# Places of one batch alternated with the route of the next, in a fused cross-attention and mixture-of-experts kernel

## The chip, the cores and the metric

The kernel runs on one core of one Trainium2 chip. The metric is the device time of one execution in microseconds (us), as the median of several runs. A core has five engines that run their own instruction streams side by side and meet only at semaphores: TensorE (PE) for matrix products, VectorE (DVE), ScalarE (ACT), GpSimd (POOL) and SyncE (SP), which here only starts DMA transfers. POOL starts transfers too, among them the indexed ones.

## What is computed

Four batches of 512 rows by 256 (`x`), a context of four times 1601 rows by 512, and a list of patch lengths. First the rows are normed and joined with a projection and with a decayed sum over the context rows, which each row of `x` picks by an index worked out from the patch lengths. Then comes a mixture of eight experts, of which every row uses the two with the largest logits:

```python
x = x + _L0_xattn_ref(_layernorm(x), ctx_2048, mask_BxS2_if0, W_in, b_in, g_res, g_init)
x = x + _L0_ffn_ref(_layernorm(x), gate_w, w1, w3, w2)

# in _L0_xattn_ref: rmsnorm, projection, then
plug = jnp.clip(jnp.cumsum(boundary_mask, axis=1) - 1, 0, plen - 1)
depool_out = depool[jnp.arange(bsz)[:, None], plug]        # depool: decayed running sum

# in _L0_ffn_ref: E = 8, TOP_K = 2
probs = jax.nn.softmax(jnp.einsum('btd,de->bte', x, gate_w))
expert_weights, expert_indices = jax.lax.top_k(probs, TOP_K)
for i in range(E):
    h = silu(x @ w1[i]) * (x @ w3[i])
    out = out + (h @ w2[i]) * wi[..., None]                # wi: weight of expert i, or 0
```

## The kernel before

Every batch is four tiles of 128 rows (`TPB` is 4, `B` is 4). The program has two parts. The **head**, up to 104 us, does everything per batch and ends in a table: which rows each expert gets, in blocks of 128. The **steps** after it go over the blocks, at most 39 (37 here), and PE is busy in them nearly without a gap. The whole head must be over before the first step, since the table needs the counts of all four batches.

There is no scheduler: each engine's instructions stand in the order in which the code issues them, and an engine that waits for a semaphore holds all that stands behind. So the order of the calls in each engine's block is the schedule. A wait of an engine on its own last instruction is written out too (`wait_ge` on the count that the instruction adds to).

The parts of the head that matter here:

- DVE, from line 1019: `position(b)` makes 13 compares of 128x128 that mark where batch `b`'s patches end; `stats_first(b)` takes the statistics of `x`; `norm_first(b)` writes the scaled context rows `hp` (the tile `hmul` in the profile); `depooled(b)` takes the decayed sums out of PE's bank; `plugs()` and `plugs_end()` make the index list `plugi` for all batches; `second(b)` joins the gathered rows `dg` and the projection into `x_all` and takes statistics again; `norm_second(b)` hands on the scale with which ACT then writes `z`.
- DVE's routing: `route(b)` copies the logits, finds the top two experts and marks them (`oh`, `picked`); `places(b)` works out the weights and each row's place in its expert's list, a chain of small instructions in which nearly each waits for the one before; `place_rows(b)` (line 1002) makes eight compares of 128x128 (`lo_hot`, shown as `ctx_sb` in the profile, whose memory it reuses). Then nine further small steps, issued through `tbl`, each of which waits for the last.
- PE, from line 1429: `boundaries(b)` needs `position(b)`; `plugs()` needs `bmask`; `depool(b)` makes the decayed sums from `hp`; `turned(b)` and `router(b)` are transposes; `through_win(b)` is the projection; `logits_of(b)` and `ranks(b)` feed `route` and `places`; `lists` makes the row lists from `lo_hot`.
- POOL, from line 508: `pow1(b)` and `pow2(b)` are the powers of -1/2 for the two norms, `gather(b)` fetches `dg` with four indexed transfers of 128 rows. They stand in one queue, so a power stands behind the gathers ahead of it.
- ACT: squares of the context, the two norms, copies of the transposes, the exponential of the logits' gap.

## Time and profile before

| | us |
|---|---|
| median of 3 runs | 457.45 |
| lowest and highest | 455.36, 458.01 |
| the profiled execution, its device time | 460.46 |
| its span in the trace | 458.9 |
| first matmul of the first step | 103.98 |
| PE busy in the span | 398.2 (87%) |

The profiled execution took 3.0 us more than the median, and 1.56 us of its own time lie outside the span. All times of the rows below count from the start of that span. An idle time in square brackets is the engine's wait ahead of an instruction, with what ended it. A row that stands for several instructions starts with the first of them and gives their time in sum.

### The profile page before, as it was taken

To read this page: it belongs to the slowest core of one execution; us is meant where nothing else is said; L and a number is where in the kernel's file an instruction comes from. 1 tells how busy PE (TensorE), PEld (TensorE's weight loads), DVE (VectorE), ACT (ScalarE), POOL (GpSimd) and SP (SyncE) were. 2 spreads that over 40 slices of the span, in tenths; PEclk is the share of its full clock that TensorE was granted. 3 is DMA by queue.
4 is the path that set the end of the run, shared out by engine and by line. 5 is a ranking of instruction groups with operands and counts; after the bars stand their busy time and mean duration, and the time that the engine had idled before them with its cause. 6 is when DMAs were issued, how large, how long until landed. Compare 5 with 4: busy or idle time off the path is not lost.

```text
span 458.9 us, 11850 instructions
## 1 busy us (share of the span) xinstructions
PE 398.2 (87%) x2269; PEld 339.4 (74%) x2270; DVE 313.5 (68%) x835; ACT 193.4 (42%) x334; POOL 204.6 (45%) x215
## 2 busy tenths in 40 slices
PE   0769895239899999999999999999999999799973
PEld 0548674127678888888888888888888888688862
DVE  7977789989685577547767764766776557736550
ACT  2547347002643455335635543463563345443320
POOL 6436456123343465235645553565565232504222
PEclk9979996557999999999999999999999999979977
DMA  6944996601895789557886986797797645525532
GB/s 188 341 161 138 296 365 193 223 25 56 253 270 171 194 250 251 182 156 205 254 255 189 270 256 158 196 277 239 194 282 242 156 138 162 147 69 153 142 105 24
DMA packets 79130, 89.79 MB, mean 196 GB/s; under 512 B 6871, under 2 KB 59351, under 8 KB 79111
## 3 DMA queue, kind: packets, MB, share of 16 engines
q1 hardware_dynamic: 64279, 55.23, 37.1%
q0 software_dynamic: 14832, 34.35, 29.5%
q8 instruction: 6, 0.10, 0.1%
q14 instruction: 13, 0.11, 0.1%
HBM read 58.76 MB, written 30.80 MB: 195 GB/s over the span
## 4 chain that ended last, share of the span: by engine, by line
PE 71%; DVE 15%; issue 5%; POOL 4%; DMA 1%; ACT 1%; DVEq 1%; ACTq 0%; POOLq 0%; SPq 0%
PE bank L1477 68%; POOL dg L499 3%; DVE onehot_lo L852 2%; PE bank L1484 2%; DVE ctx_sb L1008 1%; ACT split L342 1%; DMA out<-yblk,itok 1%; POOL rs L489 1%; PE bank L1425 1%; DVE hmul L901 1%; DVE st L927 1%; DVE st L874 1%; DVE x_all L924 1%; DVE topi L949 1%; DVE x_all L918 1%
## 5 line engine op out<-in xcount | busy, mean ns | idle before, releaser
L1477 PE MATMUL bank<-split,xT_hi 128*128 x592 | 171.7, 412 | 7.4 <-DVE split L348 3.3
L1477 PEld LDWEIGHTS bank<-split,xT_hi 128*128 128x128 f32 x592 | 108.6, 193 | 31.7 <-issue 9.4
L1477 PEld LDWEIGHTS bank<-split,hT 128*128 128x128 f32 x888 | 112.9, 193 | 4.3 <-ACT yblk L714 0.9
L1477 PE MATMUL bank<-split,hT 128*128 (+1 forms) x888 | 114.2, 285 | 0.8 <-ACT yblk L714 0.7
L544 POOL DMA_INDIRECT out<-yblk,itok x37 | 76.6, 2071 | 75.0 <-ACT yblk L714 67.4
L707 ACT ACTIVATE gact<-bank 128x512 f32<-128x512 f32 x74 | 44.3, 599 | 148.4 <-PE bank L1477 148.4
L1207 DVE TENSOR_TENSOR hmul<-gact,bank 128x512 f32<-128x512 f32 x74 | 50.8, 687 | 78.5 <-ACT gact L707 78.3
L1477 PE MATMUL bank<-split,xT_lo 128*128 x296 | 94.8, 402 | 0.0
L536 POOL DMA_INDIRECT xblk<-z_rows,gidx x40 | 41.3, 1032 | 90.7 <-DVE gidx L1246 83.1
L348 DVE TENSOR_TENSOR split<-raw,split x22 | 50.4, 2293 | 28.4 <-ACT split L342 28.4
L1477 PEld LDWEIGHTS bank<-split,xT_lo 128*128 128x128 f32 x296 | 57.1, 193 | 13.8
L1215 DVE STREAM_TRANSPOSE swap_in<-hmul 128x512 f32<-128x512 f32 x74 | 52.7, 712 | 4.4
L1223 DVE TENSOR_TENSOR hT<-swap_out,hT 128x512 fp32r<-128x512 f32 x72 | 48.9, 680 | 1.5
L342 ACT ACTIVATE split<-raw (+1 forms) x24 | 45.8, 1914 | 9.7 <-issue 6.3
L281 POOL DMA_DIRECT2D raw<-in_L_ffn_w x56 | 38.0, 683 | 26.0 <-issue 26.0
L695 ACT ACTIVATE hT<-swap_out 128x512 fp32r<-128x512 f32 x72 | 45.1, 627 | 2.3 <-issue 2.3
L714 ACT ACTIVATE yblk<-bank,wtok 128x256 f32<-128x256 f32 x37 | 17.2, 465 | 35.5 <-PE bank L1477 35.5
L284 POOL DMA_DIRECT2D raw<-in_L_ffn_w x28 | 20.7, 747 | 11.7 <-issue 10.5
L689 ACT ACTIVATE xT_hi<-bank 128x256 fp32r<-128x256 f32 x38 | 14.4, 378 | 18.2 <-PE bank L1484 18.2
L499 POOL DMA_INDIRECT dg<-depool_rows,plugi x16 | 16.8, 1050 | 10.9 <-DVE plugi L867 6.8
L1484 PE MATMUL bank<-ident,xblk 128*128 128x128 f32 x76 | 15.1, 281 | 1.1 <-DVE table L1178 1.1
L1484 PEld LDWEIGHTS bank<-ident,xblk 128*128 128x128 f32 x76 | 11.0, 146 | 6.7 <-DMA xblk<-z_rows,gidx 1.3
(196 smaller groups left out, 325.4 us busy)
## 6 DMA issues: line engine op xcount, KB each, us to landing
raw<-in_L_ffn_w POOLq DMA_DIRECT2D x84, 256.0 KB
swap_rows<-swap_in SPq DMA_DIRECT2D x74, 256.0 KB, 3.1
swap_out<-swap_rows SPq DMA_DIRECT2D x74, 256.0 KB, 3.2
ctx_sb<-in_ctx SPq DMA_DIRECT2D x4, 1024.0 KB, 6.3
raw<-in_L_ffn_w SPq DMA_DIRECT2D x12, 256.0 KB, 6.6
x_all<-in_x SPq DMA_DIRECT2D x4, 512.0 KB, 8.3
depool_rows<-gact SPq DMA_DIRECT2D x4, 512.0 KB, 3.6
out<-x_all SPq DMA_DIRECT2D x4, 512.0 KB, 7.1
```

Source lines behind the costliest of these rows:

```text
L281: eng.dma_start(raw_up[:, ds(slot, 1), m, n >> 1, cols], rows).then_inc(signal, 16)
L342: act.activation(split_chunk[:, ds(raw3 * 2 + m, 1)], raw_chunk[:, ds(raw3 + m, 1)], ACT.Copy)\
L348: dve.tensor_tensor(split_chunk[:, ds(raw3 * 2 + m + 3, 1)], raw_chunk[:, ds(raw3 + m, 1)], split_chunk[:, ds(raw3 * 2 + m, 1)].bitcast(f3 ...
L536: pool.indirect_dma_start(xblk[:, q, :], None, z_dram[:, :], bass.IndirectOffsetOnAxis(ap=gidx[:, q:q + 1], axis=0))\
L544: pool.indirect_dma_start(out[:, :], bass.IndirectOffsetOnAxis(ap=itok[:, q:q + 1], axis=0), yblk[:, q, :], None, compute_op=ALU.add).then ...
L695: act.activation(hT_hi[:, q, ks].rearrange("p k (a t) -> p a k t", a=NQ), swap_out[:, q, part], ACT.Copy)\
L707: act.activation(gact[:, half * HALF:(half + 1) * HALF], p_gate[half][:, :], ACT.Silu)\
L1207: dve.tensor_tensor(hmul[:, cols], gact[:, cols], p_lin[part][:, :], ALU.mult)\
L1215: dve.transpose(swap_in[:, q, part].rearrange("p b k t -> p k b t"), hmul[:, part * HALF:(part + 1) * HALF].rearrange("p (k b t) -> p k b ...
L1223: dve.tensor_tensor(hT_lo[:, q, ks].rearrange("p k (a t) -> p a k t", a=NQ), swap_out[:, q, part], hT_hi[:, q, ks].bitcast(f32).rearrange( ...
L1477: mm = pe.matmul(out_, xp, w_, start=start and n == 0, stop=stop and n == 2)
L1484: mm = pe.transpose(p_xT[:, k * P:(k + 1) * P], xblk[:, q, k * P:(k + 1) * P], ident[:, :])
```

## The change

Four things are moved; nothing is computed that was not computed before.

1. On DVE, the scaled rows of batch 1 (`norm_first(1)`) stand ahead of its last `position(3)`, and `stats_first(2)` and `depooled(1)` stand ahead of `plugs()`. On PE, `depool(1)` stands ahead of `boundaries(3)`, and `turned(1)` ahead of `plugs()`. On POOL, `gather(0)` stands whole behind `pow1(2)`, where before two of its tiles stood ahead.
2. `places(0)` and `route(1)` become one sequence, `places_beside_route(0)`, in which instructions of the two alternate; so do `places(1)` and `route(2)`.
3. The 32 row compares are made by `next_rows(count)`, which gives out the next ones by a running number. Fewer stand in a row: six at first, ten in `places(2)`, four behind it, four in `route(3)`, six in `tbl` and two behind it. Each compare now adds to the semaphore, where the last of four did.
4. In `places(2)` and `places(3)` the weights stand behind the positions.

```diff
-            gather(0, range(0, PAIRS))
             pow1(2)
-            gather(0, range(PAIRS, TPB))
+            gather(0)
             pow1(3)
...
+            def next_rows(count):
+
+                for n in range(rows_made[0], rows_made[0] + count):
+                    b, r, j = n // (2 * TPB), n // TPB % 2, n // (2 * TPB) * TPB + n % TPB
+                    if n % (2 * TPB) == 0:
+                        dve.wait_ge(s["rank_ready"], 5 * (b + 1))
+                    dve.tensor_scalar(lo_hot[:, r * B * TPB + j, :], iota_b[:, :], rank_lof[:, r, j:j + 1],
+                                      None, ALU.is_equal).then_inc(s["lohot_ready"], 1)
+                rows_made[0] += count
...
+            def places_beside_route(b):
+
+                denominator(b)
+                logits_out(b + 1)
+                first_weight(b)
+                positions(b)
+                largest(b + 1)
+                second_weight(b)
+                next_base(b)
+                own_positions(b)
+                experts_of(b + 1)
+                summed(b)
+                gap_of(b + 1)
+                experts_as_floats(b + 1)
+                whole(b)
+                choices(b + 1)
+                parts(b)
+                picks(b + 1)
+                low_part(b)
+
+            def places(b, rows):
+
+                positions(b)
+                denominator(b)
+                next_rows(rows)
+                next_base(b)
+                own_positions(b)
+                first_weight(b)
+                next_rows(rows)
+                summed(b)
+                second_weight(b)
+                next_rows(rows)
+                whole(b)
+                next_rows(rows)
+                parts(b)
+                next_rows(rows)
+                low_part(b)
...
             depooled(0)
+            norm_first(1)
             position(3)
-            norm_first(1)
+            stats_first(2)
+            depooled(1)
             plugs()
             scale_win()
             plugs_end()
-            stats_first(2)
-            depooled(1)
             norm_first(2)
...
-            places(0)
+            places_beside_route(0)
             norm_second(2)
-            route(1)
             second(3)
...
-            place_rows(0)
+            next_rows(6)
             norm_second(3)
-            places(1)
-            route(2)
-            places(2)
-            place_rows(1)
-            place_rows(2)
-            route(3)
-            places(3)
+            places_beside_route(1)
+            places(2, 2)
+            next_rows(4)
+            route(3, 1)
+            places(3, 0)
...
-            for b in range(1, B):
-                boundaries(b)
+            boundaries(1)
+            boundaries(2)
+            depool(1)
+            boundaries(3)
+            turned(1)
             plugs()
-            depool(1)
-            turned(1)
             through_win(0)
...
-            pe.wait_ge(s["lohot_ready"], 2 * B)
+            pe.wait_ge(s["lohot_ready"], N_LIST)
```

PE's queue from `turned(0)` (the first `ident,batch` row) to `turned(1)` and the projection: `onehot` rows are `boundaries`, 13 matmuls for one batch; `bmask` rows are `plugs`; `hmul` rows are `depool`. Before:

```order
L1348 MATMUL bank<-ident,batch 128x128 x8
L1328 MATMUL bank<-onehot_hi,onehot_lo 128x4 x39
L1337 MATMUL bank<-bmask,tri_b 128x16
L1338 MATMUL bank<-bmask,ident_b 128x16
L1341 MATMUL bank<-bmask,ones_b 128x4x3
L1341 MATMUL bank<-bmask,ones_b 128x4x2
L1341 MATMUL bank<-bmask,ones_b 128x4
L1360 MATMUL bank<-hmul,decayT 128x256 x2
```

and now:

```order
L1427 MATMUL bank<-ident,batch 128x128 x8
L1407 MATMUL bank<-onehot_hi,onehot_lo 128x4 x26
L1439 MATMUL bank<-hmul,decayT 128x256 x2
L1441 MATMUL bank<-hmul,decayT 128x256
L1439 MATMUL bank<-hmul,decayT 128x256
L1441 MATMUL bank<-hmul,decayT 128x256
L1439 MATMUL bank<-hmul,decayT 128x256
L1441 MATMUL bank<-hmul,decayT 128x256
L1407 MATMUL bank<-onehot_hi,onehot_lo 128x4 x13
L1427 MATMUL bank<-ident,batch 128x128 x8
L1416 MATMUL bank<-bmask,tri_b 128x16
...
L1461 MATMUL bank<-win,batch 128x256 x8
```

`depool(1)` went up past `boundaries(3)` and past `plugs`, which in its turn now also stands behind `turned(1)`.

DVE's queue from `depooled(0)` (`gact`) on: `onehot_lo` is `position(3)`, `nb` and `hmul` are `norm_first(1)`, `bmask` to `plugi` are the two plug functions with the scaling of `win` between, `st` to `vin` are `stats_first(2)`. Before:

```order
L909 TENSOR_TENSOR gact<-bank,bin 128x512 x2
L852 TENSOR_SCALAR onehot_lo<-iota_b,ln_v 128x128 x13
L893 SCALAR_TENSOR_TENSOR nb<-mv,rs 128x4
L901 SCALAR_TENSOR_TENSOR hmul<-ctx_sb,rs,ginit 128x256 x4
L859 TENSOR_SCALAR bmask<-bank 128x16
L1016 TENSOR_SCALAR win<-bank,gres 128x256 x2
L864 TENSOR_SCALAR plugf<-bank 128x16
L867 TENSOR_SCALAR plugi<-plugf 128x16
L874 BN_STATS st<-x_all 128x6 x4
L877 BN_AGGR mv<-st 128x2 x4
L881 TENSOR_SCALAR vin<-sumsq 128x4
L885 TENSOR_SCALAR vin<-mv 128x4
```

and now:

```order
L908 TENSOR_TENSOR gact<-bank,bin 128x512 x2
L892 SCALAR_TENSOR_TENSOR nb<-mv,rs 128x4
L900 SCALAR_TENSOR_TENSOR hmul<-ctx_sb,rs,ginit 128x256 x4
L851 TENSOR_SCALAR onehot_lo<-iota_b,ln_v 128x128 x13
L873 BN_STATS st<-x_all 128x6 x4
L876 BN_AGGR mv<-st 128x2 x4
L880 TENSOR_SCALAR vin<-sumsq 128x4
L884 TENSOR_SCALAR vin<-mv 128x4
L908 TENSOR_TENSOR gact<-bank,bin 128x512 x2
L858 TENSOR_SCALAR bmask<-bank 128x16
L1097 TENSOR_SCALAR win<-bank,gres 128x256 x2
L863 TENSOR_SCALAR plugf<-bank 128x16
```

The plug indices went down past the statistics of batch 2 and past `depooled(1)`, and the scaled rows went up past 13 compares.

DVE's queue behind `second(2)`: places of batch 0 (`den` to `rank_lof`), then route of batch 1, whose first row is the last that stands here. Before:

```order
L971 TENSOR_SCALAR den<-egap 128x4
L973 RECIPROCAL wts<-den 128x4
L975 TENSOR_TENSOR wts<-egap,wts 128x4
L980 TENSOR_TENSOR posf<-bank,base 128x32
L984 TENSOR_TENSOR base<-base,bank 128x8
L988 TENSOR_TENSOR posm<-oh,posf 128x32 x2
L991 TENSOR_REDUCE blk<-posm 128x2x4
L993 CAST rank<-blk 128x2x4
L995 TENSOR_SCALAR rank_lo<-rank 128x2x4
L997 TENSOR_SCALAR rank_hi<-rank 128x2x4
L1000 CAST rank_lof<-rank_lo 128x2x4
L943 COPY logits<-bank 128x32
```

and now:

```order
L992 TENSOR_SCALAR den<-egap 128x4
L959 COPY logits<-bank 128x32
L996 RECIPROCAL wts<-den 128x4
L1006 TENSOR_TENSOR posf<-bank,base 128x32
L955 MAX top<-logits 128x8 x4
L1000 TENSOR_TENSOR wts<-egap,wts 128x4
L1012 TENSOR_TENSOR base<-base,bank 128x8
L1018 TENSOR_TENSOR posm<-oh,posf 128x32 x2
L964 MAX_INDEX topi<-top,logits 128x8 x4
L1023 TENSOR_REDUCE blk<-posm 128x2x4
L967 TENSOR_TENSOR gap<-top 128x4
L973 CAST topf<-topi 128x8
```

Between an instruction of places and the next that waits for it now stands one of the route, and the other way round.

## Rows read from the trace of the kernel before

**Rows 1.** Busy time by stretch: us and count by engine, granted clock, DMA share, GB/s.

```profile
25.00:30.00 5.00, 2.00 (x21) 1.70 (x22) 4.97 (x23) 3.20 (x8) 0.22 (x1) 0.74 0.40 115
30.00:35.00 5.00, 5.00 (x17) 4.01 (x16) 2.38 (x11) 0.00 (x0) 4.50 (x4) 0.58 0.69 256
```

**Rows 2.** Timeline of DVE: start us, us, engine, line, operation, [idle before].

```profile
24.49 2.19 DVE L852 TENSOR_SCALAR onehot_lo<-iota_b,ln_v 128x128 bf16<-128x128 bf16 x13
...
28.26 0.16 DVE L859 TENSOR_SCALAR bmask<-bank 128x16 bf16<-128x16 f32 x1
...
29.40 1.40 DVE L874 BATCH_NORM_STATS2 st<-x_all 128x6 f32<-128x256 f32 x4
...
31.25 0.17 DVE L885 TENSOR_SCALAR vin<-mv 128x4 f32<-128x4 f32 x1
...
34.70 0.69 DVE L909 TENSOR_TENSOR gact<-bank,bin 128x512 f32<-128x512 f32 x1 [2.37 <-PE bank L1362]
```

**Rows 3.** Timeline of POOL, 29 to 46 us.

```profile
29.78 1.10 POOL L499 DMA_INDIRECT dg<-depool_rows,plugi  x1 [6.77 <-DVE plugi L867]
...
39.06 1.67 POOL L489 TENSOR_TENSOR rs<-vin,neg_half 128x8 f32<-128x8 f32 x1 [2.75 <-DVE vin L885]
40.92 1.01 POOL L499 DMA_INDIRECT dg<-depool_rows,plugi  x1 [0.19 <-issue]
...
44.77 1.59 POOL L499 DMA_INDIRECT dg<-depool_rows,plugi  x1 [0.30 <-issue]
```

**Rows 4.** Timeline of PE, 33 to 82 us.

```profile
35.37 3.62 PE L1382 MATMUL bank<-win,batch 128*128 128x256 f32 x16
...
41.85 1.04 PE L1348 MATMUL bank<-ident,batch 128*128 128x128 f32 x8
...
69.82 1.92 PE L1402 MATMUL bank<-gate,batch 128*128 128x8 f32 x16
75.44 2.07 PE L1348 MATMUL bank<-ident,z 128*128 128x128 f32 x8 [3.70 <-ACT z L635]
78.46 0.21 PE L1411 MATMUL bank<-picked,tri_b 128*128 128x32 bf16 x1 [0.95 <-DVE picked L963]
...
78.69 3.56 PE L1402 MATMUL bank<-gate,batch 128*128 128x8 f32 x16
```

**Rows 5.** Timeline of DVE, 44 to 54 us: joining of batches 0 and 1.

```profile
44.31 1.22 DVE L918 TENSOR_TENSOR x_all<-x_all,dg 128x1024 f32<-128x1024 f32 x1
...
53.01 1.23 DVE L918 TENSOR_TENSOR x_all<-x_all,dg 128x1024 f32<-128x1024 f32 x1 [2.92 <-DMA dg<-depool_rows,plugi]
```

**Rows 6.** Landing of `dg`, last tile of gather(1), issued at 44.77.

```profile
DMA to landing us min/median/max: 8.2/8.2/8.2
```

**Rows 7.** Landing of `dg`, last tile of gather(3), issued at 62.94.

```profile
DMA to landing us min/median/max: 5.8/5.8/5.8
```

**Rows 8.** Timeline of DVE, 64 to 69 us: places(0), route(1), start of second(3).

```profile
64.89 0.17 DVE L934 TENSOR_SCALAR vin<-mv 128x4 f32<-128x4 f32 x1
64.97 0.16 DVE L971 TENSOR_SCALAR den<-egap 128x4 f32<-128x4 f32 x1
65.17 0.18 DVE L973 RECIPROCAL wts<-den 128x4 f32<-128x4 f32 x1
...
68.79 1.22 DVE L918 TENSOR_TENSOR x_all<-x_all,dg 128x1024 f32<-128x1024 f32 x1
```

**Rows 9.** Timeline of DVE, 78 to 84 us.

```profile
78.87 0.19 DVE L980 TENSOR_TENSOR posf<-bank,base 128x32 f32<-128x32 f32 x1
...
82.84 0.18 DVE L943 COPY logits<-bank 128x32 f32<-128x32 f32 x1
```

**Rows 10.** Timeline of DVE, 86 to 90 us: table, last compares, first use.

```profile
86.64 0.17 DVE L1073 TENSOR_SCALAR n_i<-base 128x8 int32<-128x8 f32 x1
...
88.81 1.39 DVE L1008 TENSOR_SCALAR ctx_sb<-iota_b,rank_lof 128x128 bf16<-128x128 bf16 x8
90.11 0.87 DVE L1092 TENSOR_TENSOR onehot_lo<-iota_f,blk 128x688 bf16<-128x688 f32 x1
```

More of the change, by code:

```diff
@@ L489, in pow1, with gather @@
                 pool.tensor_tensor(rs[:, b % 2], vin[:, :], neg_half[:, :], ALU.pow).then_inc(s["rs_ready"], 1)
-            def gather(b, tiles=range(TPB)):
+            def gather(b):
                 pool.wait_ge(s["plug_ready"], 1)
@@ L496, in gather @@
                     pool.wait_ge(s["xd_ready"], b - 1)
-                for j in tiles:
+                for j in range(TPB):
                     n = b * TPB + j
@@ L939, in norm_second, with largest @@
                    .then_inc(s["nb2_ready"], 1)
-            def route(b):
-                dve.wait_ge(s["logit_mm"], b + 1)
-                dve.tensor_copy(logits[:, :, :].rearrange("p j e -> p (j e)"), p_logit).then_inc(s["logit_ready"], 1)
+            rows_made = [0]
+            def next_rows(count):
[6 more added lines that the diff above has]
+                rows_made[0] += count
+            def largest(b):
                 dve.wait_ge(s["logit_ready"], b + 1)
@@ L946, in route, with logits_out, experts_of @@
                     dve.max(top[:, j, :], logits[:, j, :]).then_inc(s["top_ready"], 1)
+            def logits_out(b):
+                dve.wait_ge(s["logit_mm"], b + 1)
+                dve.tensor_copy(logits[:, :, :].rearrange("p j e -> p (j e)"), p_logit).then_inc(s["logit_ready"], 1)
+            def experts_of(b):
                 dve.wait_ge(s["top_ready"], TPB * (b + 1))
@@ L961, in route, with picks, denominator, first_weight @@
                                   ALU.is_equal).then_inc(s["oh_ready"], 1)
+            def picks(b):
                 dve.wait_ge(s["oh_ready"], b + 1)
[L963 removed]
+                dve.tensor_tensor(picked[:, :, :], oh[:, 0, tiles_of(b)], oh[:, 1, tiles_of(b)], ALU.add)\
                    .then_inc(s["picked_ready"], 1)
[L966 to L968 removed]
+            def denominator(b):
                 dve.wait_ge(s["egap_ready"], b + 1)
                 dve.tensor_scalar(den[:, :], egap[:, :], 1.0, None, ALU.add).then_inc(s["den_ready"], 1)
+            def first_weight(b):
                 dve.wait_ge(s["den_ready"], b + 1)
[L973 removed]
+                dve.reciprocal(wts[:, 0, tiles_of(b)], den[:, :]).then_inc(s["wts_ready"], 1)
+            def second_weight(b):
                 dve.wait_ge(s["wts_ready"], 2 * b + 1)
[L975 removed]
+                dve.tensor_tensor(wts[:, 1, tiles_of(b)], egap[:, :], wts[:, 0, tiles_of(b)], ALU.mult)\
                    .then_inc(s["wts_ready"], 1)
+            def positions(b):
                 dve.wait_ge(s["rank_mm"], b + 1)
@@ L992, in places, with whole, parts @@
+            def whole(b):
                 dve.wait_ge(s["rank_ready"], 5 * b + 1)
-                dve.tensor_copy(rank[:, :, tiles], blk[:, :, tiles]).then_inc(s["rank_ready"], 1)
+                dve.tensor_copy(rank[:, :, tiles_of(b)], blk[:, :, tiles_of(b)]).then_inc(s["rank_ready"], 1)
+            def parts(b):
                 dve.wait_ge(s["rank_ready"], 5 * b + 2)
-                dve.tensor_scalar(rank_lo[:, :, tiles], rank[:, :, tiles], P - 1, None, ALU.bitwise_and)\
+                dve.tensor_scalar(rank_lo[:, :, tiles_of(b)], rank[:, :, tiles_of(b)], P - 1, None, ALU.bitwise_and)\
@@ L1002, in place_rows @@
-            def place_rows(b):
-                tiles = slice(b * TPB, (b + 1) * TPB)
-                dve.wait_ge(s["rank_ready"], 5 * (b + 1))
-                for r in range(2):
-                    for j in range(b * TPB, (b + 1) * TPB):
-                        ins = dve.tensor_scalar(lo_hot[:, r * B * TPB + j, :], iota_b[:, :], rank_lof[:, r, j:j + 1],
-                                                None, ALU.is_equal)
-                    ins.then_inc(s["lohot_ready"], 1)
+                dve.tensor_copy(rank_lof[:, :, tiles_of(b)], rank_lo[:, :, tiles_of(b)]).then_inc(s["rank_ready"], 1)
@@ new lines, in route @@
+            def route(b, rows=0):
+                logits_out(b)
+                next_rows(rows)
+                largest(b)
+                next_rows(rows)
+                experts_of(b)
+                gap_of(b)
+                experts_as_floats(b)
+                next_rows(rows)
+                choices(b)
+                next_rows(rows)
+                picks(b)
+            def places_beside_route(b):
[16 more added lines that the diff above has]
+                low_part(b)
@@ new lines, in places @@
+            def places(b, rows):
[5 more added lines that the diff above has]
+                first_weight(b)
+                next_rows(rows)
+                summed(b)
+                second_weight(b)
+                next_rows(rows)
+                whole(b)
+                next_rows(rows)
+                parts(b)
+                next_rows(rows)
+                low_part(b)
```

44 lines of the change are left out of this document (24 added, 20 removed).

## Prediction

> **What bounds the kernel now.** I read the table of times first: PE is busy for 87% of the span, and its first step starts at 103.98 us. From there the steps run on PE nearly without a gap, and no instruction of theirs is touched. So the change acts on the head, and each us by which the head ends earlier moves all the steps: I take it as 1 to 1. Next I read the timelines of the head, to see which wait ends last at each place. Three stretches come out. Up to 53 us DVE, PE and POOL wait for one another in turn: POOL for the plug indices [rows 3], DVE for the decayed sums of batch 1 [rows 2] and for the gathered rows of batch 1 [rows 5]. From 30 to 35 PE had 0.58 of its clock granted [rows 1], so mostly its lower level, 1.2 instead of 2.4 GHz. From 53 to 69 us DVE joins, and routes between. From 69 us to the lists DVE alone has the path: small instructions, each waiting for the last, and 32 compares.
>
> **Change 1, the early order.** DVE's `position(3)` starts at 24.49 and takes 2.2; `norm_first(1)` then runs until `bmask` at 28.26, so 1.6; `stats_first(2)` goes from 29.40 to 31.25, 1.9 with its last instruction; one half of `depooled` is 0.69, and two that wait for nothing I take as 1.2 [rows 2]. In the new order, from 24.5: scaled rows until 26.1, `position(3)` until 28.3, statistics until 30.2, `depooled(1)` until 31.4, then `bmask`. The first gather came 1.52 behind `bmask` (28.26 to 29.78) [rows 2, 3], so it now comes at 32.9, 3.1 later than before. That is the loss.
>
> The gain is on both sides of it. PE gets the first `hp` of batch 1 at 24.9 (24.5 and a quarter of 1.6), and is not held by `plugs`: seven products of `depool`. Those of batch 2 took 3.0 (from 38.8, where the 16 records from 35.37 on are issued, to 41.85) [rows 4]. So `depool(1)` is over near 28.3, and `depooled(1)` waits for nothing, where its second half waited 2.37 [rows 2]. `through_win(0)` starts with the scaled `win`, at 32.4, lasts 3.4 [rows 4], `depool(2)` 3.0: over at 38.8, 3.0 earlier than 41.85. `depooled(2)` ends at 39.5.
>
> POOL: four tiles of a gather stand 1.28 apart ((44.77 - 40.92) / 3) [rows 3], so `gather(0)` starts its last at 36.8 and ends at 37.8. `pow1(3)` stands behind it, 1.67 [rows 3], so over at 39.5 (40.7 before). Its input is there, since `stats_first(3)` no longer waits for batch 1. So DVE's `norm_first(3)` starts at 39.5, and `second(0)` 1.7 later, at 41.2, against 44.31 [rows 5]: 3.1 earlier. The last tile of `gather(0)`, issued at 36.8, has to be there by then, 4.4 later. Gathers beside little traffic are the nearest case, and I have no row for less than 5.8 beside full traffic [rows 7]; so between nothing and 1.4 is lost here, and I take nothing, since the first weights are not yet loading then.
>
> `second(1)` waited for its last tile, issued at 44.77 and landed 8.2 later [rows 3, 5, 6]. Now that tile is issued at 43.5 (39.5 + 0.2 + 3 x 1.28), and the first weights, which SP loads behind `depooled(2)`, come 2.6 to 3.0 earlier and are further along. By 5.8 [rows 7] and 8.2 [rows 6] it lands between 49.3 and 51.7. I take 50.2, a little under the middle, since the weights are ahead of it by more. So `second(1)` starts **2.8 earlier** than 53.01; the bounds are 1.3 and 3.7.
>
> **Change 2, places beside route.** An instruction that waits for nothing starts 0.08 behind the one before (64.89 and 64.97); one that waits for it starts at its end plus 0.04 (64.97 and 65.17) [rows 8]. `places(0)` and `route(1)` took 3.82 with the next norm between (64.97 to 68.79) [rows 8]. Laid out with the two spacings, the alternated sequence takes 2.42: 1.3 less. The Trainium skill, "VectorE: DVE Perf Modes", section The DRAIN you can't avoid, says that "the next op does not start until the 8-stage pipe empties", though a next one that isn't held may start earlier. The trace speaks against the first half: 0.17 long, and the next 0.08 behind [rows 8].
>
> Of the first 1.3 nothing arrives. `second(3)` starts at 68.79, and its last tile was issued at 62.94 and landed 5.8 later, at 68.74 [rows 7, 8]. That gather stands behind `pow2(1)`, thus behind `second(1)`; it moves by 2.8 and no more. So `second(3)` starts at 66.0. `norm_second(2)` comes 0.6 later than it would, behind the whole block; ACT's `z` of batch 2 has room for it.
>
> The second 1.3 is partly lost too. PE's `router(3)` is paced by ACT's `z` (75.44, 2.07 long) [rows 4]: now 72.6 to 74.7. Before, PE then waited 0.95 for `picked` of batch 2 [rows 4]. Now `picked` is done near 74.2, and `ranks(2)` starts behind the router at 74.75. The positions come 0.41 behind that (78.46 to 78.87) [rows 4, 9], at 75.2: **3.7 earlier** than 78.87. So 0.9 of 1.3 is kept. The logits of batch 2, which the block now wants second, end 2.2 later than 69.82 - 2.8 + 1.9 at most [rows 4], near 71.1, ahead of the block at 71.8.
>
> **Change 3, compares in gaps.** A compare takes 0.163 (1.39 for eight with the tail, next at 90.11 behind 88.81) [rows 10]. In `places(2)` and behind it, 14 compares are 2.3 and the rest 1.1 with hardly a wait: 3.4 from positions to the logits of batch 3, where it was 3.97 (78.87 to 82.84) [rows 9]. PE's logits of batch 3 take 3.5 behind `ranks(2)` [rows 4], so they end at the same time, at 78.6. DVE goes on at 78.6, 4.2 earlier than 82.84. `route(3)` gets four compares: gaps of 0.20 to 0.41 become 0.24 to 0.48, 0.13 in all. The table's nine steps and the compares took 3.47 (86.64 to 90.11) [rows 10]. Six compares now stand in gaps, at 0.04 to 0.06 each, 0.26; the eight took 1.30 and the wait ahead of them 0.23, in whose place stand two and 0.08, 0.41. That makes 2.61, **0.86 less**. Each compare now signals. I take that as nothing, as small instructions that signal still stand 0.08 apart [rows 8]; the other bound is 0.09 for each (0.25 alone against 0.163), 2.9 in all, and below nothing there is no reason to go.
>
> **Sum**, on the profiled execution: 2.8 (up to `second(3)`) + 0.9 (positions of batch 2) + 0.5 (logits of batch 3) - 0.1 (`route(3)`) + 0.9 (table) = 5.0 less than 460.46. The median is 3.0 below that execution. In it, all of `depool(1)` fell on the low clock [rows 1, 2]; a luckier one loses less there, so I take 0.6 off: 4.4 less than the median, **453.05**.
>
> **Rivals.** (a) PE's clock falls between `turned(1)`, over near 29.8, and `through_win(0)` at 32.4. The trace shows the fall behind such a lull: from 25 to 30 PE was busy for 2.0 of 5, the clock averaged 0.74, and 0.58 in the next 5, in which PE was busy throughout [rows 1]. The new lull is shorter, 2.6. At 1.2 GHz `through_win(0)` costs up to 3.4 more, half of that if the clock comes back midway. Then `second(0)` gains 0 to 1.4. The Trainium skill, "TensorE: Matmul & The Clock Gate", part The HAM clock gate, adds that the monitor is free-running and does not start with the kernel, so executions may differ. The same place is reached if the last tile of `gather(1)` needs 8.2 again. Either gives 1.5 less gain: 454.55. (b) The tile that holds `second(3)` lands faster, as there is less left to load: up to 1.3 more, 451.75. (c) Alternating doesn't do what it says, each small instruction still taking its full 0.2, as the page on VectorE has it: changes 2 and 3 then give nothing and 2.2 of the sum go: 455.25. The two spacings speak against it. (d) Slower: the late start of `gather(0)`. Its last tile, issued at 36.8, would hold `second(0)`, and with it all that follows. Behind `second(0)` 2.2 are gained in any case, so it decides from 46.5 on (44.31 + 2.2), 9.7 behind the issue; at 12 it would be 459.8. The longest landing seen was 8.2 [rows 6].
>
> **Chances.** Forecast 0.50; (a) 0.34; (b) 0.07; (c) 0.05; (d) 0.04. The range goes from 450.6 (b with a good landing of batch 1's rows) to 455.9 (c, or a with both its causes, and the spread of the runs). Within 0.5%, which is 2.3 us and about what a measurement of this kernel can tell from no change, lies all above 455.16: the upper part of (a) and most of (c), with the costs of signalling compares, 0.16. Slower than 459.7: 0.04. Faster by more: 0.80.
>
> **What would show it.** First gather near 32.9 and `second(0)` near 41.2 with no wait for `dg`; `depool(1)` at full clock; `second(1)` near 50.2 and still waiting for its tile; `second(3)` now waiting for a transfer, about 1.3; `ranks(2)` no longer waiting for DVE; PE's first step near 99. I am wrong if the small instructions of the mixed block stand 0.2 apart, if compares grow beyond 0.17, or if PE's low clock reaches into the projection.

## The result, and the profile after

| | before | after |
|---|---|---|
| median of 20 runs each, us | 458.28 | 455.00 |
| lowest and highest | 455.36, 462.48 | 452.44, 457.92 |
| the profiled execution, its device time | 460.46 | 454.56 |
| its span | 458.9 | 452.9 |
| first matmul of the first step | 103.98 | 99.96 |

The ratio is 0.9922, 95% interval 0.9902 to 0.9942: 0.8% faster, 3.3 us by the medians. The forecast was 4.4 less than 457.45, which is 453.05. 455.0 lies in its range, 1.95 above the forecast: 1.1 of that since less was gained, 0.8 since the median of three runs of the kernel before was lower than that of twenty.

The windows of the changed kernel, with the columns of [rows 1]: us and count of PE, PEld, DVE, ACT and POOL, granted clock, DMA share, GB/s.

```profile
25.00:30.00 5.00, 4.84 (x17) 3.79 (x18) 4.97 (x26) 3.01 (x8) 0.00 (x0) 0.66 0.82 249
30.00:35.00 5.00, 4.26 (x39) 3.65 (x38) 4.97 (x18) 4.06 (x12) 3.44 (x3) 1.00 0.54 184
...
60.00:64.00 4.00, 3.92 (x16) 3.29 (x16) 3.93 (x23) 0.00 (x0) 2.45 (x3) 0.57 1.08 387
64.00:68.00 4.00, 4.00 (x13) 3.18 (x12) 3.17 (x21) 2.17 (x5) 0.23 (x1) 0.58 0.37 134
96.00:101.00 5.00, 2.03 (x7) 1.23 (x8) 4.43 (x7) 1.67 (x2) 0.91 (x2) 0.50 0.17 51
```

PE's low clock left the stretch from 30 to 35 us [rows 1], but it is there between 25 and 30, and it came back at 60 to 68, where I had not looked for it, with PE busy for 7.92 of these 8 us. The timeline of DVE, changed kernel, answers [rows 2, 5]:

```profile
24.54 1.66 DVE L900 SCALAR_TENSOR_TENSOR hmul<-ctx_sb,rs,ginit 128x256 f32<-128x256 f32 x4
...
30.16 1.29 DVE L908 TENSOR_TENSOR gact<-bank,bin 128x512 f32<-128x512 f32 x2
...
41.45 1.21 DVE L917 TENSOR_TENSOR x_all<-x_all,dg 128x1024 f32<-128x1024 f32 x1
...
50.39 1.22 DVE L917 TENSOR_TENSOR x_all<-x_all,dg 128x1024 f32<-128x1024 f32 x1 [3.16 <-DMA dg<-depool_rows,plugi]
```

`depooled(1)` (both halves at 30.16) waits for nothing, `second(0)` starts 2.86 earlier and without a wait, `second(1)` 2.62 earlier, still behind its tile. POOL, answering [rows 3]:

```profile
32.88 1.18 POOL L499 DMA_INDIRECT dg<-depool_rows,plugi  x1 [0.92 <-DVE plugi L866]
...
43.79 0.95 POOL L499 DMA_INDIRECT dg<-depool_rows,plugi  x1 [0.30 <-issue]
```

The last of these is the tile of 50.39: 6.6 from issue to landing, between the two rows from which I had bounded it. DVE from the mixed block to the table, answering [rows 8 to 10]:

```profile
63.02 0.16 DVE L992 TENSOR_SCALAR den<-egap 128x4 f32<-128x4 f32 x1
63.09 0.18 DVE L959 COPY logits<-bank 128x32 f32<-128x32 f32 x1
63.22 0.18 DVE L996 RECIPROCAL wts<-den 128x4 f32<-128x4 f32 x1
...
65.42 0.16 DVE L937 SCALAR_TENSOR_TENSOR nb<-mv,rs 128x4 f32<-128x4 f32 x1
66.38 1.23 DVE L917 TENSOR_TENSOR x_all<-x_all,dg 128x1024 f32<-128x1024 f32 x1 [0.80 <-DMA dg<-depool_rows,plugi]
...
71.98 0.16 DVE L937 SCALAR_TENSOR_TENSOR nb<-mv,rs 128x4 f32<-128x4 f32 x1
...
76.12 0.19 DVE L1006 TENSOR_TENSOR posf<-bank,base 128x32 f32<-128x32 f32 x1 [1.20 <-PE bank L1496]
...
79.55 0.19 DVE L959 COPY logits<-bank 128x32 f32<-128x32 f32 x1
...
83.49 0.17 DVE L1152 TENSOR_SCALAR n_i<-base 128x8 int32<-128x8 f32 x1
...
86.22 0.87 DVE L1171 TENSOR_TENSOR onehot_lo<-iota_f,blk 128x688 bf16<-128x688 f32 x1
```

From `den` to the end of the block (65.42) is 2.40. `second(3)` is 2.41 earlier and waits for a transfer, the table part takes 2.73 where it took 3.47. But the positions of batch 2 (76.12) are only 2.75 earlier than in [rows 9], and DVE waits 1.20 for PE ahead of them. PE and ACT in that stretch:

```profile
61.23 6.75 PE L1461 MATMUL bank<-win,batch 128*128 128x256 f32 x16
67.82 1.04 PE L1427 MATMUL bank<-ident,z 128*128 128x128 f32 x8
...
73.83 2.07 PE L1427 MATMUL bank<-ident,z 128*128 128x128 f32 x8 [2.65 <-ACT z L634]
75.69 0.23 PE L1490 MATMUL bank<-picked,tri_b 128*128 128x32 bf16 x1
```

```profile
68.52 1.08 ACT L642 ACTIVATE batch<-bank 128x512 f32<-128x512 f32 x2 [0.73 <-PE bank L1427]
69.49 3.71 ACT L342 ACTIVATE split<-raw 128x2048 fp32r<-128x2048 f32 x2
73.09 2.07 ACT L634 ACTIVATE z<-x_all,nb,rs 128x256 f32<-128x256 f32 x4
```

One chain: `through_win(3)` runs at the low clock (6.75, against 3.70 at the high one), so the transposes of batch 2 come at 67.82, ACT copies them at 68.52, then stand two splits of the experts' weights (`split<-raw`, 3.71), and only then `z` of batch 3, whose scale is there at 72.14 (71.98 plus 0.16), starts at 73.09. In the kernel before, the same `z` still waited for DVE behind the same splits:

```profile
74.69 2.07 ACT L635 ACTIVATE z<-x_all,nb,rs 128x256 f32<-128x256 f32 x4 [0.87 <-DVE nb L938]
```

`ranks(2)` follows the router at 75.69 with no wait for `picked`, as predicted.

### The profile page after: what moved, and what is told of

The parts are those of the page before. It is cut to its first block, busy times and chain, and to the rows that moved or that the text cites. A ratio compares the mean times of both kernels' runs of the same rounds, so it can differ in the third digit from the quotient of the medians.

```text
span 452.9 us, 11848 instructions
## 1 busy us (share of the span) xinstructions
PE 397.6 (88%) x2269; PEld 339.4 (75%) x2270; DVE 309.9 (68%) x835; ACT 193.0 (43%) x334; POOL 204.8 (45%) x215
## 4 chain that ended last, share of the span: by engine, by line
PE 75%; DVE 11%; issue 4%; POOL 3%; DMA 3%; ACT 2%; DVEq 1%; ACTq 0%; POOLq 0%; SPq 0%
PE bank L1557 69%; POOL dg L499 2%; PE bank L1564 2%; DMA dg<-depool_rows,plugi 2%; ACT split L342 2%; PE bank L1461 1%; DVE onehot_lo L851 1%; DVE ctx_sb L948 1%; DMA out<-yblk,itok 1%; PE bank L1504 1%; PE bank L1439 1%; DVE st L873 1%; PE bank L1427 1%; DMA ln_i<-in_mask_BxS_if 1%; DVE split L348 1%
## 5 line engine op out<-in xcount | busy, mean ns | idle before, releaser
L535 POOL DMA_INDIRECT xblk<-z_rows,gidx x40 | 41.2, 1031 | 88.4 <-DVE gidx L1325 80.2
L1461 PE MATMUL bank<-win,batch 128*128 128x256 f32 x64 | 17.9, 442 | 0.9 <-DVE win L1097 0.5
L1461 PEld LDWEIGHTS bank<-win,batch 128*128 128x128 f32 x64 | 14.0, 224 | 3.8 <-DVE x_all L923 0.9
```

Source lines behind the costliest of these rows:

```text
L535: pool.indirect_dma_start(xblk[:, q, :], None, z_dram[:, :], bass.IndirectOffsetOnAxis(ap=gidx[:, q:q + 1], axis=0))\
L1461: mm = pe.matmul(pH[j // 2][:, (j % 2) * D:(j % 2 + 1) * D], hnT[b % 2][:, j, k * P:(k + 1) * P], win[:, k, :], start=(k == 0), stop=(k == ...
```

## Experiments

Each kernel is timed against the kernel before on the same chip, and ratios are to that; times of different chips don't compare, since the kernel before had a median of 458.29 to 459.5 on them. The quotient of two medians can differ from the ratio given by up to 0.0035. First, each half alone.

**The early order alone.** Changes 2 to 4 left out.

> The kernel before with change 1 alone: the scaled rows of batch 1 and its decayed sums ahead of the last boundaries, gather(0) whole behind pow1(2). Routing and compares as before. My theory: the early order gives what it gave in the changed kernel, since nothing late reaches back. second(0) near 41.4 and second(1) near 50.4 us, against 44.31 and 53.01; the first step starts 2.6 earlier than 103.98, near 101.4. Time 2.4 to 2.8 us below the kernel before. Rival, that most of the gain comes from the late changes: first step within 1 us of 104.

**Changes 2 to 4 alone**, with the early order of before.

> The changed kernel with the early order of the kernel before: only alternation, compares in gaps and weights behind positions are left of the change. Theory, with the parts adding up: second(1) at 53.0 as before, second(3) at 68.8 and waiting about 1.3 us for its gathered tile, the first step 2.1 earlier than 103.98 where PE's clock holds through the projection of batch 3, 1.2 to 1.5 where it doesn't. Time 1.2 to 2.1 us below the kernel before. Rival, that the small instructions of two chains don't overlap: no gain within 0.5 us.

Measured: 457.41 and 0.992 (0.989 to 0.995) for the first; 456.31 and 0.9913 (0.988 to 0.9946) for the second. First steps at 103.45 and 103.03, so 0.5 and 0.95 earlier, where 2.6 and 1.2 to 2.1 were expected. With the early order alone `second(0)` is at 41.49 and `second(1)` at 50.48, as in the whole change. What keeps the rest from the first step in this execution stands in `second(2)`. PE and DVE, early order alone:

```profile
55.18 6.72 PE L1381 MATMUL bank<-win,batch 128*128 128x256 f32 x16
```

```profile
61.93 0.69 DVE L923 TENSOR_TENSOR x_all<-x_all,bank 128x512 f32<-128x512 f32 x1 [1.90 <-PE bank L1381]
```

The low clock fell on `through_win(2)`, and DVE waited 1.90 for it. In the other kernel it fell there too (57.19, 6.52): DVE waited 2.00 in `second(2)` and 0.51 for the next logits. Its 0.95 isn't a measure of changes 2 to 4 either: its `second(1)` is at 51.77, 1.24 earlier than in [rows 5] with the same queues up to there, by a clock that rose earlier (shown under "1 to 1" below). There `z` of batch 3 was held as well, and that with `through_win(3)` at 3.70, the high clock. DVE hands on its scale, and ACT starts it 1.07 after it is there:

```profile
74.90 0.16 DVE L938 SCALAR_TENSOR_TENSOR nb<-mv,rs 128x4 f32<-128x4 f32 x1
```

```profile
72.53 3.70 ACT L342 ACTIVATE split<-raw 128x2048 fp32r<-128x2048 f32 x2
76.13 2.06 ACT L635 ACTIVATE z<-x_all,nb,rs 128x256 f32<-128x256 f32 x4
```

By the ratios the halves add up to twice the whole (by the quotients of the medians, 0.9955 and 0.9931, to about one and a half); intervals of 0.3% to either side can't weigh parts of 0.3 to 0.6%, so what follows reads parts from traces, and uses times only where they stand well apart.

**Without alternation.** Places and route one behind the other, as before; all else as changed.

```diff
-            places_beside_route(0)
+            places_apart(0)
             norm_second(2)
+            route(1)
```

> The changed kernel with places(0) and route(1), and places(1) and route(2), one behind the other as before, while the early order and the compares in gaps stay. Theory: alternation hides 1.3 us twice, but the first is taken by the wait for the gathered tile of batch 3 (0.80 seen), and of the second the wait of DVE for PE's ranks (1.20 seen) takes most. So the time is 0 to 0.6 us above the changed kernel, with DVE's wait ahead of second(3) gone and the positions of batch 2 within 0.6 us of 76.1. Rival, that alternation carries the late gain: 2.6 us slower than the changed kernel.

Measured: 456.94, 0.9938 (0.9905 to 0.997). `second(3)` starts at 66.59 without a wait, 0.2 behind the changed kernel's: the first block's gain is indeed lost to the transfer. At the second block PE waits for `picked` again, as in [rows 4]:

```profile
73.12 2.07 PE L1441 MATMUL bank<-ident,z 128*128 128x128 f32 x8 [2.96 <-ACT z L634]
76.31 0.21 PE L1504 MATMUL bank<-picked,tri_b 128*128 128x32 bf16 x1 [1.11 <-DVE picked L987]
```

The first step comes at 100.57, only 0.6 behind 99.96, since in the changed kernel's execution `z` was held, and here it was not (72.38, behind a wait of 0.20 for DVE). By time the two kernels can't be told apart (0.9938 and 0.9922). Two more executions are without that hold.

**Splits late.** ACT's two splits stand behind `z` and the transposes of batch 3.

```diff
-            first_hi(0)
-            first_hi(1)
...
+            first_hi(0)
+            first_hi(1)
```

> The changed kernel with ACT's two splits of the first weights (3.6 us, 69.5 to 73.1 in its trace) moved behind the norm and the transposes of batch 3, where ACT waits anyway. Theory: in the changed kernel these splits held ACT's z of batch 3 by 1.0 us (73.09 against nb at 71.98), so positions of batch 2 came at 76.12 instead of 75.0. Now z starts near 72.2, positions near 75.1, and the first step up to 0.9 us earlier where PE's clock was low in the projection of batch 3; where it was not, ACT is free anyway and the gain is 0 to 0.4. Time 0.3 to 0.9 us below the changed kernel. Rival, that DVE alone sets the end there: no difference.

Measured: 453.75, 0.9855 (0.982 to 0.9889). ACT:

```profile
72.14 2.08 ACT L634 ACTIVATE z<-x_all,nb,rs 128x256 f32<-128x256 f32 x4 [3.69 <-DVE nb L937]
...
75.49 3.70 ACT L342 ACTIVATE split<-raw 128x2048 fp32r<-128x2048 f32 x2
```

`z` now waits for DVE and not for ACT, positions of batch 2 are at 75.20 and the first step is at 99.20. In this execution all four projections took 3.70 or 3.72.

**The changed kernel a second time**, on another chip, to see whether the low clock belongs to it.

> The changed kernel itself, beside the two above on one chip. Theory (a low clock in the head comes in some executions and not in others): 1 to 2 us above the two kernels above, 454.5 to 455.5 us, and if through_win(3) is 3.7 us in this profiled execution, posf of batch 2 stands near 75.0 with the wait for TensorE under 0.6 us, where it was 76.12 with 1.20. Rival (the low clock belongs to this kernel's order of work): through_win(3) over 6 us again.

Measured: 455.19, 0.9917 (0.989 to 0.9943). PE, and ACT under it:

```profile
53.17 5.39 PE L1461 MATMUL bank<-win,batch 128*128 128x256 f32 x16
...
61.61 3.70 PE L1461 MATMUL bank<-win,batch 128*128 128x256 f32 x16
```

```profile
68.61 3.70 ACT L342 ACTIVATE split<-raw 128x2048 fp32r<-128x2048 f32 x2
72.25 2.07 ACT L634 ACTIVATE z<-x_all,nb,rs 128x256 f32<-128x256 f32 x4
```

The same kernel, the same work, and here the clock was low on `through_win(2)`, where DVE was waiting for a tile anyway. The splits fit in exactly (end and `z` at 72.25), positions stand at 75.31 and the first step at 99.31. Beside the kernel without alternation (100.57) that makes the alternation worth 1.26, against 0.9 predicted; 0.14 of it is `second(3)`, which starts later there (66.59 against 66.45).

What decides on the hold is how far apart the two scales come, and the low clock on `through_win(3)` is only one part of it. From `z` of batch 2 to the end of the splits ACT needs 6.7 us when nothing holds it (65.51 to 72.25 here). DVE hands on the scale of batch 3 5.6 behind the start of `second(3)`. In the kernel before, `route(1)` stood between the scale of batch 2 and `second(3)`, 1.96 us (66.83 to 68.79), and ACT had 0.87 left. The alternation puts `route(1)` ahead of that scale, so the splits now fit only if `second(3)` waits a full us for its tile. It waited 0.97 here (hold 0.04), 0.80 in the first trace (hold 0.95: 0.22 of this kind, and the 0.73 that ACT waited for PE), and in the two alternated traces with early splits where it waited for nothing, changes 2 to 4 alone and the gather split below, `z` was held for 1.07 and 0.91 with `through_win(3)` at 3.70. In the trace with matmuls ahead of the step it waited 1.24; there `through_win(3)` ran low in part (5.17), and nothing was held. Between the two traces of the changed kernel, the longer hold goes with 0.65 at the first step (99.96 against 99.31).

**Compares in bulk.** The 32 compares stand in rows of 8, 16 and 8.

```diff
-            next_rows(6)
+            next_rows(8)
...
-            places(2, 2)
-            next_rows(4)
-            route(3, 1)
+            places(2, 0)
+            next_rows(16)
+            route(3, 0)
```

> The changed kernel with the 32 compares in bulk: eight behind second(3), sixteen behind places(2), eight behind the table's blocks, as in the kernel before; alternation and early order stay. Theory: eight compares cost 1.30 in bulk and 0.6 to 0.7 in the gaps of the table, two more of them stand ahead of norm_second(3) at no cost, and in places(2) they cost 0.3 more in bulk. From n_i to the first hi_eq it takes 3.47 again, instead of 2.73; n_i comes 0.2 to 0.6 later. Time 1.0 to 1.4 us above the changed kernel. Rival, that compares between small steps slow these as much as they save: within 0.3 us of the changed kernel.

Measured: 455.11, 0.9937 (0.991 to 0.9964). DVE:

```profile
74.99 0.19 DVE L1006 TENSOR_TENSOR posf<-bank,base 128x32 f32<-128x32 f32 x1 [0.56 <-PE bank L1496]
...
76.36 2.68 DVE L948 TENSOR_SCALAR ctx_sb<-iota_b,rank_lof 128x128 bf16<-128x128 bf16 x16
78.96 0.18 DVE L959 COPY logits<-bank 128x32 f32<-128x32 f32 x1
...
82.76 0.17 DVE L1152 TENSOR_SCALAR n_i<-base 128x8 int32<-128x8 f32 x1
...
86.23 0.87 DVE L1171 TENSOR_TENSOR onehot_lo<-iota_f,blk 128x688 bf16<-128x688 f32 x1
```

From positions to logits 3.97 again, from `n_i` to the first use 3.47 again; with compares in gaps it was 3.42 to 3.58 and 2.73 to 2.75. Behind sixteen compares that all signal the next instruction starts 2.60 later, 0.163 each, as with one signal in four [rows 10]: signalling is free. The first step is at 100.10, 0.9 later than 99.20, the nearest trace with the clock equally high (that of late splits, whose positions were 0.2 later, so 1.1 in all); 1.3 was predicted for change 3 with `route(3)`: the two shares seen are 0.4 (3.97 to 3.56) and 0.7, less 0.1 in `route(3)`. By time it is not told apart from the changed kernel (0.9922).

**The gather split as before**, two tiles ahead of `pow1(2)`.

```diff
-            pow1(2)
-            gather(0)
+            gather(0, range(0, PAIRS))
+            pow1(2)
+            gather(0, range(PAIRS, TPB))
```

> The changed kernel with POOL's queue as before: two tiles of gather(0) ahead of pow1(2), two behind it. The plug indices now come at 32.5, so the power of batch 2 waits for them behind two gathers. Theory: pow1(2) at 35.3 instead of 30.3, norm_first(2) of DVE near 37.0 instead of 32.5, so second(0) near 45.5 to 46 instead of 41.4, and the first step 3.5 to 4.5 later than in the changed kernel, about where the kernel before has it or later. Time 3.0 to 4.5 us above the changed kernel. Rival, that the wait for the tiles of gather(1) sets second(1) whatever the power does: less than 1.5 us above it.

Measured: 455.93, 0.9946 (0.9915 to 0.9977). With the first gather at 32.88, the power behind two tiles holds DVE; `second(0)` is 2.8 later, the first step (102.28) 2.3:

```profile
36.99 0.16 DVE L893 SCALAR_TENSOR_TENSOR nb<-mv,rs 128x4 f32<-128x4 f32 x1 [4.39 <-POOL rs L489]
```

I had expected more, 3.5 to 4.5: the second hold, for `pow1(3)`, was only 0.59. But `second(0)` and `second(1)` are at 44.22 and 53.24, where the kernel before has them (44.31 and 53.01): the move of the gather is no small part of change 1 but its condition.

**Unread matmuls in the head.** Twelve of 512 columns between the transposes and the logits of batches 0 and 1; nobody reads them.

```diff
+            def warm(count, to=3):
+                for _ in range(count):
+                    pe.matmul(bank[to][:, :].rearrange("p (j d) -> p j d", d=P), ident_b[:, :],
+                              iota_b[:, :].unsqueeze(1).broadcast_to([P, 4, P]), start=True, stop=True)
```

> The changed kernel with 12 matmuls of 128x512 (bf16) whose result nobody reads, in PE's queue between the transposes of z and the logits of batches 0 and 1: three behind router(0), four behind logits_of(0), five behind router(1). Theory: PE's clock fell in the head (through_win(3) took 6.75 us at half clock instead of 3.70) behind a stretch of transposes paced by ACT and of matmuls of 8 columns. With these between, the granted clock stays at 1.0 from 34 to 66 us, both projections take 3.7, and the first step starts where the changed kernel has it with its clock up, 0.9 to 1.1 before 99.96, near 99.0. Time 0.3 to 1.2 us below the changed kernel, since not each of its runs loses it. Rival, that the clock falls all the same, or that the added matmuls delay the projections by what they save: no difference.

**Unread matmuls ahead of the first step**, fourteen of them.

> The changed kernel with 14 matmuls of 128x512 (bf16) on PE whose result nobody reads, in its idle time ahead of the first step: nine behind the lists, two behind the matmul of the words, three behind the first transposes. Theory: the first step ran at half clock for 5 us (99.96 to 104.9), which costs half of that. With PE kept busy from 92 on, the granted clock is up at 1.0 when the first step starts, or rises within 2 us of it. The first step starts within 0.3 us of 99.96, and the time is 1.2 to 2.6 us below the changed kernel. Rival, that the first step is held by DVE's and ACT's splits and not by PE's clock: within 0.5 us of it.

Measured: 453.88, 0.9914 (0.9875 to 0.9953) with those in the head: projections 3.62 and 3.70, `z` held by no more than 0.1, positions at 74.95, first step at 98.96. Ahead of the step: 453.79, 0.9918 (0.9886 to 0.9951). PE at the step, the second kernel:

```profile
98.93 1.19 PE L1565 MATMUL bank<-split,xT_hi 128*128 x4 [0.99 <-DVE xT_lo L1279]
...
107.84 1.19 PE L1565 MATMUL bank<-split,xT_hi 128*128 x4 [0.91 <-DVE xT_lo L1279]
```

and the changed kernel there:

```profile
99.96 2.07 PE L1557 MATMUL bank<-split,xT_hi 128*128 x4 [1.39 <-DVE xT_lo L1279]
...
110.15 1.20 PE L1557 MATMUL bank<-split,xT_hi 128*128 x4
```

At the high clock four such matmuls take 1.19 instead of 2.07, and the first step is 8.9 long, not 10.2. The second one now waits 0.91 for DVE, so of 2.2 that were to be had (1.3 and 0.91) the 0.91 are given back. Neither time is clearly below the changed kernel's.

**All together.** Late splits with the matmuls ahead of the step, and with both groups of matmuls.

> The changed kernel with two additions: ACT's two weight splits of batches 2 and 3 stand behind the normalisation of batch 3, and 14 matmuls of 512 columns whose result nobody reads stand on TensorE ahead of the first step of the stream. Theory (the splits held z of batch 3, and the half clock of the first step is worth something by itself): first step near 99.2 as with the splits moved alone, its matmuls at the full clock, and the stream's end 1 to 3 us earlier than with either alone; 452 to 453 us, 0.4 to 1 under the kernel with the splits moved alone. Rival (the stream is given back: the second step waits for DVE's splits of xT whatever the clock of the first): first step 99.2, full clock, but the time of the splits moved alone, 453.8 give or take 0.5.

> The former kernel, and 12 more unread matmuls of 512 columns between the transposes and the logits of batches 0 and 1. Theory (a low clock in the head is what cost the changed kernel about 0.7 us beside the splits): all projections of the window halves 3.6 to 3.7 us in this execution, first step 98.7 to 99.2, 452 to 453 us. Rival (the clock in the head is up anyway once the splits are late, and the added matmuls lie beside ACT's copies): the same time as the former kernel within 0.4 us.

Measured: 451.58, 0.9859 (0.9819 to 0.9899), and 452.77, 0.9878 (0.9844 to 0.9911), where the changed kernel had 455.19 on the same chip. So these two and the late splits alone are the fastest kernels here. That the added matmuls give something over the late splits (0.9855) no ratio shows, and none excludes it: the rival is not refuted. In the first of the two the low clock came to the head (`through_win(2)` 6.73): DVE waited 0.22 and 0.50 for PE, then for its tile not at all, and the first step is at 98.87. There the fourteen matmuls did not hold the clock over the first step either: its first four took 1.97. In the second kernel they took 1.19.

**Late splits, no alternation.**

> The changed kernel with ACT's two weight splits behind the normalisation of batch 3, and places and route one behind the other: what the alternation is worth once neither the splits nor a slow projection stand ahead of the positions of batch 2. Theory (0.9 of the second block's 1.3 arrive there, as predicted): ranks of batch 2 wait for DVE again, about 0.9, positions of batch 2 near 76.1 and first step near 100.1, where the kernel with alternation has 75.2 and 99.2; 454.6 us. Rival (the alternation is hidden in any case, as in the profiled pair without late splits, where it was 0.6): first step 99.2 to 99.5, 453.8 us. For the late splits: by the medians of the run with them alone, 0.9855 of the kernel before; if they carry that much by themselves, this kernel too is at 0.989 or below; if the head's 0.1 to 0.8 us is all of it, at 0.992 to 0.993.

Measured: 455.52, 0.9939 (0.9913 to 0.9966). PE:

```profile
32.37 5.41 PE L1475 MATMUL bank<-win,batch 128*128 128x256 f32 x16 [0.50 <-DVE win L1109]
...
55.38 6.47 PE L1475 MATMUL bank<-win,batch 128*128 128x256 f32 x16
...
77.94 0.21 PE L1504 MATMUL bank<-picked,tri_b 128*128 128x32 bf16 x1 [1.11 <-DVE picked L987]
```

The wait for `picked` is back, 1.11, as the theory says. But this execution is no clean pair for the rest: here, and in this trace alone, `through_win(0)` ran low, and `second(1)` is at 51.69 instead of 50.39, the first step at 102.19. The ratio, 0.8% above that of late splits with alternation, is more than the 1.26 us (0.3%) of the traces. And late splits gained 0.7% over the changed kernel's ratio (the intervals don't meet), where two traces of it show 0.1 and 0.8 us in the head. That late splits help where places and route alternate is clear; why by so much is open. Without alternation they gave nothing by the ratios, 0.9939 against 0.9938, which fits the account of the hold, since there `z` was not held. It doesn't prove it: the intervals are 0.3% to either side, and the quotients of the medians differ by that (0.9915 and 0.9944). So the alternation and the place of the splits have to be judged together: by the ratios the alternation is worth 0.8% with the splits late (0.4% by the quotients of the medians), and 0.2%, within the noise, with them early.

| kernel | low clock in the head on | first step at | span behind that |
|---|---|---|---|
| before | - | 103.98 | 354.9 |
| changed, first and second trace | `through_win(3)`; (2) | 99.96; 99.31 | 352.9; 355.1 |
| early order alone | (2) | 103.45 | 352.5 |
| changes 2 to 4 alone | (2) | 103.03 | 351.1 |
| no alternation; also splits late | (2); (0) and (2) | 100.57; 102.19 | 352.8; 350.3 |
| splits late | - | 99.20 | 352.9 |
| compares in bulk | - | 100.10 | 349.6 |
| gather split | (2) | 102.28 | 352.7 |
| matmuls in the head | - | 98.96 | 353.2 |
| matmuls ahead of the step | (3) | 98.93 | 351.3 |
| late, with step; with both | (2); - | 98.87; 99.13 | 351.6; 350.7 |

## Why the prediction held, point by point

- **First gather 32.9, `second(0)` 41.2 with no wait.** 32.88 and 41.45. Right; the working of change 1 held term by term, and the late gather of rival (d) never showed a wait.
- **`depool(1)` at full clock.** Wrong: the clock averaged 0.66 from 25 to 30. It cost nothing, since DVE had position, statistics and then `depooled(1)` at 30.16, late enough. I had tied the fall in [rows 1] to the lull ahead of it; with the lull shorter the low stretch came earlier and did not go.
- **`second(1)` 50.2, 2.8 earlier.** 50.39, 2.6 earlier; landing 6.6 inside 5.8 to 8.2.
- **Block 2.42.** 2.40, so rival (c) falls. The Trainium skill, "VectorE: DVE Perf Modes", section The DRAIN you can't avoid, has the next operation wait for the emptied pipe, and adds that a next one that is not held starts earlier. Here `den` (0.16) starts at 63.02 and the copy behind it at 63.09, before it ends, and the reciprocal that needs `den` at 63.22, while the copy still runs. So the trace agrees with the second half, and a full wait behind every operation it does not show.
- **`second(3)` 66.0, waiting 1.3.** 66.38, waiting 0.80. The tile was not slower to land (5.4 against 5.8) but later to be issued: at 61.00, 1.94 before 62.94 and not 2.8, since `second(1)` gained 2.6 and the issue ahead of it took 1.93 instead of 1.26. The sum had moved the gather as a whole.
- **Positions of batch 2 at 75.2.** 76.12 in the first trace: this is the step that failed, the sentence that ACT's `z` of batch 2 "has room". I had followed `z` of batch 2 and not what stands behind it in ACT's queue, the two splits of 3.71, ahead of `z` of batch 3. ACT's queue had 0.87 us left there, and moving `route(1)` ahead of `norm_second(2)` takes 1.96 away; only the wait of `second(3)` gives some back. In the second trace the splits just fit and the positions were at 75.31, in the trace with late splits at 75.20. The sum had the block's delay as free, and at the high clock too it has no margin.
- **Logits of batch 3 at 78.6, `route(3)` 0.1 longer, table 0.86 less.** 79.55 (78.87 in the second trace); 3.94 against 3.80, 0.14 longer; 0.74 less. Right, but for what the positions brought along.
- **First step near 99.** 99.96 and 99.31: 4.0 and 4.7 of the 5.0.
- **Rival (a)** named the mechanism in the wrong place. `through_win(0)` ran low in one of the twelve traces with the new early order. `through_win(2)` or `(3)` did in nine of all fourteen traces, behind transposes paced by ACT's copies and logits of 8 columns, and in neither of the two kernels whose head has unread matmuls ahead of them; what sets the place in the other twelve is open, and two traces are few, since three of the twelve have no low projection either. That 455.0 lies near (a)'s 454.55 is luck: the clock of `through_win(0)`, which gave that number, was high (3.72). The clock is of two levels, 1.2 and 2.4 GHz, and 0.57 is mostly the lower. The Trainium skill, "TensorE: Matmul & The Clock Gate", part The HAM clock gate, has the monitor free-running, so that executions differ; the two traces of the changed kernel agree, 6.75 and 3.70 for the same projection.
- **1 to 1.** The profiled pair differs by 5.9, of which the head is 4.0. The last column of the table shows the same steps at 349.6 to 355.1. PE's clock goes with that. Whole steps of the second trace of the changed kernel, and of the kernel with compares in bulk, in the columns above:

```profile
99.31:454.40 355.09, 338.36 (x1890) 290.68 (x1890) 225.15 (x404) 151.72 (x245) 157.88 (x147) 0.97 0.69 190
```

```profile
100.10:449.70 349.60, 332.49 (x1890) 287.07 (x1890) 225.05 (x404) 151.68 (x245) 158.14 (x147) 0.99 0.69 193
```

The same 1890 matmuls keep PE busy 5.9 longer, and the other engines are busy alike. Read in windows of 5 us, the clock falls in the first step, near 400 us and in the last 25 us. As an estimate from these windows, (1 - granted clock) times length, summed: 9.2 to 12.0 us are missing in the five traces at 352.8 to 355.1 (the kernel before has 12.0, the changed one 9.2), 7.2 to 7.7 in three at 352.5 to 353.2, and 2.8 to 6.6 in the six at 349.6 to 351.6. So 2.0 of the pair's 5.9 (354.9 less 352.9) are steps that the change doesn't touch, and one profiled execution is no measure to a us.

The 0.6 that I took off for a luckier one was too little: the medians differ by 3.3. The head's gain of 4.0 and 4.7 is above that by 0.7 and 1.4, and here the kernel before had bad luck too. The kernel with changes 2 to 4 alone has the queues of the kernel before up to `second(1)`, and in its execution the clock rose within `depool(1)`. DVE, answering the last of [rows 2]:

```profile
33.70 0.69 DVE L909 TENSOR_TENSOR gact<-bank,bin 128x512 f32<-128x512 f32 x1 [1.34 <-PE bank L1442]
```

`second(0)` is at 43.31 there and `second(1)` at 51.77, 1.0 and 1.24 earlier than in [rows 5]. Against such an execution the change gains 1.4 up to `second(1)` and not 2.6. How often either comes, two traces can't say. That 455.0 is close to the number of (c) says nothing for (c).

## What to carry to other kernels

Two chains of small dependent instructions on DVE, laid one into the other, cost little more than one; the gain arrives only where nothing else is late, so price the next wait at each block (here nothing at the first, about 1.2 us at the second). When an instruction is moved later by half a us, follow the queue of the engine that it feeds to the next piece that the critical chain needs, and put long work that isn't due (3.7 us of splits) behind it. A schedule that is worked out at PE's high clock should be read again with each lone projection at the low one.

## What was not expected of the hardware

- The low clock comes to a PE that the profile shows as busy: 7.92 of 8 us at 0.57 and 0.58 in the windows from 60 to 68 us. It also differs between executions. The 40 slices of the second trace of the changed kernel (tenths of full clock), and under it those of the kernel with compares in bulk:

```profile
PEclk9989896558999999999999999999999999889967
```

```profile
PEclk9999995559999999999999999999999999999989
```

- Both are at or near half clock in slices 7 to 9 (68 to 102 us), up to the first step. They differ in the head, and again at the end, which goes with 355.1 and 349.6 behind the first step.
- Fourteen unread matmuls held the clock up over DVE's part in two of three traces: four matmuls of the first step in 1.19 us, not 2.07. In the third it fell again from 96 to 100 us, and they took 1.97.
